# Filler matmuls on TensorE at the end of the first mixture layer's overflow code and behind the next layer's first transposes

## The reference

```python
x = x + diffusion_gnn(ln(x), edges, W, b, weights)        # three diffusion steps
x = x + moe_ffn(ln(x))         # 8 experts, 2 per token: gelu(x @ we1[e]) @ we2[e]
x = x + gru_gnn(ln(x), edges, edge_attr)
x = x + moe_lstm(ln(x))        # 8 experts, 2 per token
# gru_gnn(h):
m   = relu(concat(h[src], edge_attr) @ W1.T + b1) @ W2.T + b2    # 4352 edges
agg = segment_sum(m, dst)
r, z, n = gates(agg @ W_ih.T + b_ih, h @ W_hh.T + b_hh)
h   = (1 - z) * n + z * h;  return h + batch_norm(h)
```

## Time and profile before

| | us |
|---|---|
| median of 3 runs | 453.43 |
| the three runs | 451.28, 453.43, 453.88 |
| the profiled execution | 456.47 |
| its span, first to last instruction | 454.7 |
| TensorE matmuls busy in it | 421.7 (93%) |
| VectorE busy | 389.3 (86%) |
| ScalarE busy | 296.2 (65%) |

### The profile page before, as it was taken

One profiled execution on the slowest core, in us unless ns is written; L12 is line 12 of the kernel. 1 busy time (PEld: TensorE's weight loads), 2 busy tenths in 40 slices (PEclk: granted clock), 3 DMA queues, 4 the chain that ended last, 5 costly groups with the idle time before them and its releaser, 6 DMA issues.

```text
span 454.7 us, 6251 instructions
## 1 busy us (share of the span) xinstructions
PE 421.7 (93%) x2239; PEld 344.8 (76%) x2239; DVE 389.3 (86%) x624; ACT 296.2 (65%) x346; POOL 124.5 (27%) x141
## 2 busy tenths in 40 slices
PE   4989999999999996797899999999999999998994
PEld 2655788888887876586799998857788778786884
DVE  6978689998899776787899987879999998898784
ACT  7865377778777763442444454558798888877552
POOL 7984010111100014147586600032001220200500
PEclk9998999999999999699999999999999999999998
DMA  7932467899998864997567504235989999988801
GB/s 232 343 106 90 186 236 306 327 331 401 361 372 309 343 229 136 370 361 246 163 208 267 149 1 185 99 138 174 385 336 341 356 379 381 353 329 322 296 24 50
DMA packets 26213, 116.20 MB, mean 256 GB/s; under 512 B 7084, under 2 KB 8268, under 8 KB 15296
## 3 DMA queue, kind: packets, MB, share of 16 engines
q1 hardware_dynamic: 18672, 93.78, 54.8%
q0 software_dynamic: 7216, 21.79, 14.9%
q10 hardware_dynamic: 288, 0.15, 0.1%
HBM read 109.15 MB, written 6.55 MB: 254 GB/s over the span
## 4 chain that ended last, share of the span: by engine, by line
PE 58%; DVE 22%; DMA 9%; ACT 4%; issue 3%; SPq 1%; POOL 1%; DVEq 0%; ACTq 0%; POOLq 0%
PE bank L1705 10%; PE bank L1706 9%; PE bank L1712 9%; DVE wlo L1048 8%; DMA xg<-node_rows,idx 6%; PE bank L2158 4%; PE bank L2156 3%; PE bank L1696 3%; PE bank L1697 3%; PE bank L1698 3%; DVE wlo L1053 2%; PE bank L1721 2%; PE bank L2044 2%; ACT whi L722 1%; PE bank L1970 1%
## 5 line engine op out<-in xcount | busy, mean ns | idle before, releaser
L1048 DVE TENSOR_TENSOR wlo<-raw,whi 128x2048 fp32r<-128x2048 f32 x72 | 163.1, 2288 | 14.8 <-ACT whi L722 13.7
L722 ACT ACTIVATE whi<-raw 128x2048 fp32r<-128x2048 f32 x73 | 138.2, 1915 | 6.3 <-PE bank L2125 5.4
L1705 PE MATMUL bank<-whi,xe_hi 128*128 128x512 f32 (+1 forms) x200 | 78.0, 393 | 1.0 <-ACT xe_hi L755 0.7
L1706 PE MATMUL bank<-wlo,xe_hi 128*128 128x512 f32 (+1 forms) x200 | 76.1, 383 | 0.0
L665 POOL DMA_INDIRECT xg<-node_rows,idx x14 | 19.9, 1424 | 140.2 <-DVE idx L1343 140.2
L1712 PE MATMUL bank<-whi,xe_lo 128*128 128x512 f32 (+1 forms) x200 | 51.9, 381 | 0.2 <-DVE xe_lo L1336 0.2
L1705 PE MATMUL bank<-whi,hT_hi 128*128 128x512 f32 (+1 forms) x124 | 46.9, 385 | 1.3 <-ACT hT_hi L785 1.1
L698 POOL DMA_INDIRECT gath<-node_rows,src_i x34 | 40.8, 1199 | 19.6 <-DVE mp L1616 9.3
L1706 PE MATMUL bank<-wlo,hT_hi 128*128 128x512 f32 (+1 forms) x124 | 45.0, 369 | 0.0
L1705 PEld LDWEIGHTS bank<-whi,xe_hi 128*128 128x128 f32 x200 | 37.6, 188 | 8.9 <-ACT xe_hi L755 0.9
L1007 ACT ACTIVATE m_hi<-mp 128x512 fp32r<-128x512 f32 x34 | 21.5, 633 | 34.2 <-PE bank L2158 14.7
(11 more groups left out here) (327 smaller groups left out, 879.2 us busy)
## 6 DMA issues: line engine op xcount, KB each, us to landing
raw<-in_weights_dram SPq DMA_DIRECT2D x85, 1024.0 KB, 6.5
y_rows<-y_sb POOLq DMA_DIRECT2D x16, 256.0 KB, 6.0
ea<-in_ea_dram SPq DMA_DIRECT2D x8, 256.0 KB
node_rows<-xn POOLq DMA_DIRECT2D x4, 256.0 KB, 2.4
gath<-node_rows,src_i POOLq DMA_INDIRECT x34
x<-in_x_dram SPq DMA_DIRECT2D x1, 512.0 KB, 4.0
gw<-in_L_ffn_gw_dram SPq DMA_DIRECT2D x1, 512.0 KB, 9.4
node_rows<-A_sb POOLq DMA_DIRECT2D x2, 256.0 KB, 5.8
```

Source lines behind the costliest of these rows:

```text
L722: act.activation(whi[n % SPL][:, :, :], raw[n % RAW][:, :, :], ACT.Copy).then_inc(hi_cut, 1)
L1048: dve.tensor_tensor(wlo[n % SPL][:, :, :], raw[n % RAW][:, :, :], whi[n % SPL][:, :, :].bitcast(f32), ALU.subtract).then_inc(lo_cut, 1)
L1705: pe.matmul(ps, xh[:, blocks + k, :], whi[w % SPL][:, k, cs], start=first and k == 0, stop=False)
L1706: pe.matmul(ps, xh[:, blocks + k, :], wlo[w % SPL][:, k, cs], start=False, stop=False)
```

## The change

Eight fillers into bank 7 stand at the end of `last_sum` of the first mixture layer only, so in each of the three branches for a last job, of which one runs. Three fillers into bank 7 stand between the transposes of tile 0 and the first product of the third layer. Nothing is removed, no wait and no signal is added, and the other engines' streams are the same.

```diff
@@ -2013,6 +2013,8 @@
                                             skip_group_check=True)
                             if run.layer == 0 and h == 1 or run.layer == 1 and n == NT - 1:
                                 ins.then_inc(tile_ps, 1)
+                    if run.layer == 0:
+                        keep_busy(B[7], 8)
 
                 def second_product(e):
                     pe.wait_ge(run.hT_hi, run.turned(e))
@@ -2103,6 +2105,7 @@
 
 
             turn_x(2, (0,))
+            keep_busy(B[7], 3)
             q = CHUNK[("gnn", "W1")]
             has_chunk(q)
             for n in range(NT):
```

## The result

| | before | changed |
|---|---|---|
| median, us | 453.65 (4 runs, 451.28 to 455.5) | 460.99 (4 runs, 456.88 to 462.55) |
| ratio, 95% interval | | 1.0131 (1.009 to 1.0171) |
| profiled execution, span | 456.47, 454.7 | 459.50, 457.7 |

The forecast was 452.9 within 450.7 to 454.8, and no measurable change. The time lies outside that range, above it. Ratios and their intervals leave out executions that are over 1.5% slower than the fastest of the same kernel, medians take in all, and a ratio is not the quotient of the two medians (here that would be 1.016). A later measurement of the same two kernels, on another occasion, gave 1.0094 (1.0061 to 1.0127), with medians of 457.91 and 454.59.

A forecast was written before the change was run, and what follows sets the result against it. TensorE's speed from 183.87 us on, at half clock until 189.4, was taken to be on the critical path. Fillers cost nothing, a gain of 0.5 (bounds 0 to 1.5): 453.43 - 0.5 = 452.9 us, range 450.7 to 454.8.

The forecast's parts named there:

- Where the time goes: In 182 to 193 us TensorE's clock halves from 182.6 to 189.4, costing transposes and product 2.2 us at most.
- the upper bound of 1.5: Most that full clock from the first transposes on could gain at the kernel's end, in us; VectorE keeps the rest.
- Eight fillers cost nothing: Eight fillers after the last sum take 1.75 us, 179.1 to 180.9, covered by TensorE's wait for `xn` till 183.87.
- late-jump rival: Sequencer jumps only after the fillers ran, ending near 184.7; transposes late, 1.1 us more, 454.5 us; chance 0.10.
- the second jump: Branch ahead of the first transposes, 250 ns at 182.2, through at 182.4; wait for `xn` hides it with 1.4 us to spare.
- shifted code: Shifted code or another DMA order might push the time beyond the 1% band: chance 0.05 for faster, 0.03 for slower.
- Does the clock hold: Deciding term: whether the 2.9 us of idling left before the transposes drops TensorE's clock; gain between 0 and 1.5 us.
- partial gain: The forecast case: clock falls before the transposes but returns sooner, gaining 0.5 us, 452.9 us; chance 0.50.
- the forecast's own sign: Clock windows in 182 to 190 us showing a fall with a return before 189 would confirm the forecast.
- Handing on one for one: Time gained at the bias sum passes whole through the first edge gather and first `mp` to the kernel's end.

The follow-up runs named there:

- the last two runs: Kernel before plus eight fillers in the body that runs, six behind the jumps, three behind the transposes, padded to shifts 256 and 128; 453.56 and 452.21 us, ratios 0.9967 and 0.996.
- f1_twenty_one_page: Kernel before plus 20 fillers in the body that runs, 54 in each unrun body, three behind the transposes (shift 256); 458.83 us, ratio 1.0105.
- e1_code_only: Kernel before plus 12 fillers in each of the two last-job bodies that are not run, none executed (shift 48); 461.50 us, ratio 1.0101.
- e2_eight_in_first: Changed kernel with the eight fillers only in the body that runs, three behind the transposes kept (shift 16); 457.96 us, ratio 1.0032.
- e4_one_page: Changed kernel's eleven executed fillers, with 60 fillers in each of the two unrun bodies (shift 256); 455.18 us, ratio 0.9983.
- f2_shift_128: Changed kernel's eleven executed fillers, with 28 fillers in each of the two unrun bodies (shift 128); 455.59 us, ratio 0.9989.
- e3_three_only: Kernel before plus only the three fillers behind the transposes; 455.11 us, ratio 0.9975.
- h1_six_one_page: Kernel before plus eight fillers in the body that runs, six behind the jumps, three behind the transposes, 57 in each unrun body (shift 256); 453.56 us, ratio 0.9967.
- g1_six_behind_jump: Kernel before plus eight fillers in the body that runs only, six behind the jumps ahead of the transposes, three behind them; 457.10 us, ratio 1.0076.

## Why the prediction was wrong

**Where the time goes: right.** The slice, the two clock levels and what a low clock costs in it were read rightly. With the clock held, the distance from the last sum's second half to the bias sum of tile 1 fell from 193.70 - 178.56 = 15.14 us to 13.88 and 13.49 in the last two runs, a gain of 1.3 and 1.7 us against the upper bound of 1.5. Averaged over the executions that a ratio counts, the granted clock was 0.994 to 0.995 in these two and 0.987 in the kernel before beside them, so the clock was higher in more than the one trace.

**Eight fillers cost nothing: right as far as they are run.** They end within the wait for `xn`, and the sequencer ran ahead over them: the jump started at 178.8. The late-jump rival named the right place, but its mechanism needs more fillers, 20 as `f1_twenty_one_page` shows, and eight don't do it.

**The step that failed** is the price of the second jump. I took the 0.25 us of line 348 over from the kernel before ("it is through at 182.4") as if it belonged to the jump. It belonged to where the code lay. I had even written that the price hangs on where the target lies and not on the number of fillers, and then let that count against the rival, although fillers are code and in three bodies move the target. The sum had no term for it, and what I gave for "shifted code" was 0.03. It is 5.62 - 0.25 = 5.4 us, of which 1.5 us were hidden by the wait for `xn` (183.87 - 182.4); 0.5 us came on top, since the second jump began at 182.7 and not at 182.2. 5.4 - 1.5 + 0.5 = 4.4 us of delay, beside the 4.45 measured. `e1_code_only` gives the whole loss without a filler run.

**Does the clock hold: not decided by the change; the runs without the delay bear the partial gain out in the trace, not in the time.** With 2.9 us of idling left it fell in each of the three runs with eight fillers and a short jump (`e2_eight_in_first`, `e4_one_page`, `f2_shift_128`), as I had thought more likely. But it was low for 3.4 us in each (183.3 to 186.7 in `e4_one_page`) and not for 6.8 (182.6 to 189.4) as before. That is the forecast's own sign, a fall with a return before 189. In `e4_one_page` and `f2_shift_128` the sum for the bias of tile 1 came 14.34 us after the last sum's second half and not 15.14, a gain of 0.8 us where I gave 0.5, a value picked between two bounds; in `e2_eight_in_first` its stall took that away (15.13). The times show nothing of it (1.0032, 0.9983, 0.9989), and 0.8 us is 0.2%, less than these intervals can tell. What the eight fillers have in it is open: `e3_three_only`, with three alone, has 14.31 us, though its clock was low for 6.8 us, from 180.1 to 186.9. In one trace of a run, when the clock happened to fall counts as much as the fillers.

**Handing on one for one: not shown by one trace.** The delay is 4.06 us at the sum and 3.79 at the first `mp`, which looks like it. But the distance between these two, 15.51 us before and 15.24 in the changed kernel, is anything from 13.78 (`e2_eight_in_first`) to 16.64 (`h1_six_one_page`) in other traces, so the close agreement is in part luck. What is handed on shows in the ratios: 1.0131, 1.0101 and 1.0094 are 5.9, 4.6 and 4.3 us, and the interval of each holds the 4.4 us of delay (1.0097). The 7.3 us between the first two medians, of four runs each, are within that noise.

## What to carry to other kernels

In a stream with jumps, adding instructions anywhere ahead of a jump's target moves the target, even into branches that never run. So before a small edit there is costed, look up how long each branch takes, how much waiting hides it and whether a DMA burst begins just then; after it, look at the branches again, since idle time may be put down to another engine. A control with the same code and nothing more executed tells an effect of place from one of work in one run; the reverse control, all the work with the code padded back to where it lay, is worth having too.

## What the runs showed of the hardware that was not expected

- The long jumps of TensorE cost 3.2 to 3.9 us without weight loads ahead of their block and 5.6 to 6.0 with them; all other branches of these lines took 0.07 to 0.43.
- The block after the one jumped into isn't there at once: at the edge, 8, 18 and 34 instructions behind the first transpose, TensorE stalled for 2.61, 0.86 and 0.44 us, the less the later it was wanted. It went on 5.4 to 6.0 us after the end of the jump before.
- TensorE's sequencer got past eight fillers at once and not past 20, where its jump began 1.0 us late.
- With 2.9 us of idling the clock fell in three runs (up to 0.8 us after the engine had begun again), and not with holes of 1.3 to 1.8 us that had fillers around them; but in `g1_six_behind_jump` it fell 1.3 us into a longer one.
